# Row tile 0's scales loaded first, the identity added in PSUM by TensorE, the adapter product masked before its split

## What is computed

```
# block 1: a fake-quantised linear layer with a low-rank term
delta = lora_B @ lora_A * 0.5                      # 1024 x 1024, rank 64
wg    = (weight + delta) in groups of 128 columns
norm  = wg / exp(scale_log)                        # one scale per row and group
q     = cb[searchsorted(thresholds, norm)]         # 8 levels
w_eff = (((q - norm) + norm) * scale) + delta
x     = x + x @ w_eff.T
# block 2: gated MLP, F = 2752, with one adapter of rank 16 per sequence
gate  = x @ W_gate.T + 0.5 * (x @ A_gate[i].T) @ B_gate[i].T
up    = the same with W_up, A_up, B_up
down  = (silu(gate) * up) @ W_down.T + adapter
x     = x + down
```

## Time and profile before

| | |
|---|---|
| median of 3 runs | 1642.22 us (1639.8 to 1643.66) |
| the profiled execution | 1641.95 us, its span 1640.4 us |
| TensorE busy | 1595.8 us, 97% |
| VectorE busy | 1284.3 us, 78% |
| ScalarE busy | 572.9 us, 35% |
| GpSimd busy | 528.8 us, 32% |
| mean granted clock of TensorE | 0.99 |

### The profile page before, as it was taken

The page is one execution under the profiler, slowest core; times in us unless marked ns, Lnnn a source line. Parts: engine busy times, 40 slices in busy tenths (PEclk is TensorE's granted clock), DMA queues, the critical chain, the costliest instruction groups (busy, mean ns, idle before and its releaser), DMA issues.

```text
span 1640.4 us, 21380 instructions
## 1 busy us (share of the span) xinstructions
PE 1595.8 (97%) x7032; PEld 1300.8 (79%) x7032; DVE 1284.3 (78%) x1727; ACT 572.9 (35%) x1024; POOL 528.8 (32%) x399
## 2 busy tenths in 40 slices
PE   4999999999999999998999999999999999999999
PEld 3878887788888888766788888888778888888887
DVE  6899968788888899877887889999766576685353
ACT  4511125433333333345333333333343333233231
POOL 4230011355555555554444455556410000000000
PEclk8999999999999999998999999999999999999999
DMA  9473264466667777784446777876357777686563
GB/s 286 103 128 92 84 200 100 102 161 158 166 156 168 178 179 174 180 244 130 115 114 133 171 166 178 185 176 172 97 172 187 170 197 177 153 229 203 152 192 117
DMA packets 381452, 264.41 MB, mean 161 GB/s; under 512 B 228640, under 2 KB 302368, under 8 KB 381216
## 3 DMA queue, kind: packets, MB, share of 16 engines
q1 hardware_dynamic: 299072, 229.31, 53.8%
q10 hardware_dynamic: 80192, 27.94, 7.1%
q0 software_dynamic: 2080, 5.80, 1.8%
HBM read 167.84 MB, written 89.36 MB: 157 GB/s over the span
## 4 chain that ended last, share of the span: by engine, by line
PE 82%; DVE 14%; issue 2%; DMA 1%; ACT 1%; SPq 0%; DVEq 0%; ACTq 0%
PE bank L1746 20%; PE bankC L1746 14%; PE bankA L1746 14%; PE bank L1973 10%; PE bankA L1973 6%; PE bankC L1973 6%; PE bankT L1973 3%; DVE qsum L1542 2%; DVE xl L1257 1%; PE bankT L1793 1%; PE bankT L1794 1%; PE bankC L1758 1%; DVE qa L1527 1%; PE bank L1775 1%; DVE ts L1350 1%
## 5 line engine op out<-in xcount | busy, mean ns | idle before, releaser
L957 ACT CAST rh<-wt 128x512 fp32r<-128x512 f32 (+1 forms) x308 | 187.8, 611 | 446.3 <-PE bankA L1758 99.2
L1248 DVE TENSOR_TENSOR rl<-wt,rh 128x512 fp32r<-128x512 f32 (+1 forms) x308 | 280.9, 917 | 7.3 <-ACT rh L957 7.2
L1411 DVE TENSOR_TENSOR ll<-ll,lh 128x512 fp32r<-128x512 f32 (+1 forms) x154 | 108.2, 703 | 154.9 <-ACT lh L1066 154.4
L1746 PE MATMUL bank<-xh,rl 128*128 128x512 f32 (+1 forms) x528 | 205.7, 390 | 0.0
L1746 PE MATMUL bank<-xl,rh 128*128 128x512 f32 (+1 forms) x528 | 205.7, 390 | 0.0
L1746 PE MATMUL bank<-xh,rh 128*128 128x512 f32 (+1 forms) x528 | 205.7, 390 | 0.0
L1066 ACT CAST lh<-ll 128x512 fp32r<-128x512 f32 (+1 forms) x154 | 95.5, 621 | 269.4 <-DMA ll<-LT_d 264.1
L824 POOL TENSOR_TENSOR wt<-wt 128x512 f32<-128x512 f32 (+1 forms) x44 | 57.6, 1309 | 318.5 <-DVE wt L1242 318.5
L1746 PE MATMUL bankC<-xh,rh 128*128 128x512 f32 (+1 forms) x352 | 137.7, 391 | 2.2 <-DVE xl L1257 2.2
L1746 PE MATMUL bankC<-xl,rh 128*128 128x512 f32 (+1 forms) x352 | 137.8, 391 | 0.0
L1746 PE MATMUL bankC<-xh,rl 128*128 128x512 f32 (+1 forms) x352 | 137.7, 391 | 0.0
(11 more groups left out here) (207 smaller groups left out, 3597.6 us busy)
## 6 DMA issues: line engine op xcount, KB each, us to landing
ll<-LT_d SPq DMA_DIRECT2D x148, 256.0 KB, 2.9
wn<-in_L_cond_W_gate_dram SPq DMA_DIRECT2D x80, 256.0 KB, 5.4
wn<-in_L_cond_W_up_dram SPq DMA_DIRECT2D x80, 256.0 KB, 5.1
RT_d<-dt SPq DMA_DIRECT2D x70, 256.0 KB, 3.2
ql<-RT_d SPq DMA_DIRECT2D x70, 256.0 KB, 3.6
LT_d<-ev ACTq DMA_DIRECT2D x60, 256.0 KB, 2.6
dn<-in_L_cond_W_down_dram SPq DMA_DIRECT2D x86, 128.0 KB, 3.8
LT_d<-s2a SPq DMA_DIRECT2D x40, 256.0 KB, 4.2
```

The costliest lines, as they stand in the source:

```text
L957: nc.scalar.copy(rh[:, v % RING, 0:KH * rows], wsrc(RSRC[p], rows)).then_inc(s_hi, 1)
L1248: dv.tensor_tensor(rl[:, v % RING, 0:KH * rows], wsrc(RSRC[p], rows), rh[:, v % RING, 0:KH * rows].bitcast(f32), ALU.subtract).then_inc(s_ ...
L1411: dv.tensor_tensor(ll[0:rows, n % NL, :], ll[0:rows, n % NL, :].bitcast(f32), lh[0:rows, n % NL, :].bitcast(f32), ALU.subtract).then_inc(s ...
L1746: last = te.matmul(OUT[p][0:rows, :], a[:, u % RING, cols], b[:, OPND[p], k, :], start=k == 0 and n == 0, stop=k == KH - 1 and n == 2 and ...
```

## The change

- The transfers of `scale` are divided: row tile 0 first (`s_sc`, one transfer of 128 pieces of 32 bytes), tiles 1 to 7 after two token transfers (`s_scr`). The exponent and the reciprocal are divided in the same way; the second exponent stands in ScalarE's list after group 10, the second reciprocal inside `quantise(0)`. VectorE waits for the codebook alone before it builds the thresholds, and does the first eight of these steps ahead of the split of `lora_B`.
- `load_weight` is one transfer instead of four.
- `XFIRST` is 20 instead of 16.
- The identity is added by TensorE: `ident_add(o)` multiplies `minus2` (-2 times the identity) with `minus` in four matmuls of 32 columns into `bankD`, after VectorE has read `delta` for the quantisation and before it reads it for `eff` (new wait `s_idn`). It stands after group 12, at `g == 4` and then at `BUILD + LATER`. `QS` falls to 21.
- `LATER` is 12 for the tiles 1 to 6 and 5 for tile 7; `adapters_lo(o - 3)` stands at the beginning of `quantise(o)`; the adapters' stores are issued a tile later.
- The mask is applied in `ts_copy` (two pieces of 64x256) and `ts_sum`; `ts_hi` is four copies of 32x512 of which VectorE waits for two (`s_th`); `ts_lo` is two subtractions (`s_tlo`), and `ts_dup` on ScalarE copies them to the other two blocks. `ts_copy`, `ts_sum`, `ts_hi` and `ts_lo` of T(h, 0) stand one product earlier, `ts_hi` of T(h, 1) too.
- In the second pass `x_hi` and `x_lo` stand one product earlier.

The diff without its context and without the declarations of semaphores, indentation cut by eight:

```diff
+minus2 = place("minus2", [P, P], f32r, S0 + 75776)
...
-XFIRST = 2 * KD
-QS = 22
+XFIRST = 20
+QS = 21
...
-LATER = KD
+LATER = {o: 12 if o < KD - 1 else 5 for o in range(1, KD)}
...
         def load_weight(o):
-            for i in range(NI):
-                sp.dma_start(lw[i * Q:(i + 1) * Q, :], weight[i * DI + o * Q:i * DI + (o + 1) * Q, :]).then_inc(s_lw, 16)
+            sp.dma_start(lw[:, :], weight.rearrange("(i o r) d -> i o r d", i=NI, r=Q)[:, bass.ds(o, 1), :, :]
+                         .rearrange("i o r d -> i (o r) d")).then_inc(s_lw, 16)
-        for i in range(NI):
-            sp.dma_start(scale[i * Q:(i + 1) * Q, :, :],
-                         scale_log[i * DI:(i + 1) * DI].rearrange("(o r) g u -> r o (g u)", r=Q)).then_inc(s_cb, 16)
+        sp.dma_start(scale[:, 0, :], scale_log.rearrange("(i o r) g u -> i o r (g u)", i=NI, r=Q)[:, bass.ds(0, 1), :, :]
+                     .rearrange("i o r g -> i (o r) g")).then_inc(s_sc, 16)
         def load_nat(m):
...
+        for i in range(NI):
+            sp.dma_start(scale[i * Q:(i + 1) * Q, 1:KD, :],
+                         scale_log[i * DI + Q:(i + 1) * DI].rearrange("(o r) g u -> r o (g u)", r=Q)).then_inc(s_scr, 16)
...
-                if i == (BUILD[o] + LATER) // KD and o < KD - 1:
+                if i == (BUILD[o] + LATER[o]) // KD and o < KD - 1:
-                if i == (BUILD[o] + 28) // KD and o < KD - 1:
-                    store_adapters(o - 1)
+                if i == (BUILD[o] + 5) // KD and o > 1:
+                    store_adapters(o - 2)
...
-            nc.scalar.copy(tx[:, :], (bankC[:, 1, :], bank1[:, :])[t][2 * CR:4 * CR, :]).then_inc(s_tq, 1)
+            for b in range(CB):
+                part = slice(b * SEQ, (b + 1) * SEQ)
+                ins = nc.scalar.activation(tx[:, part], (bankC[:, 1, :], bank1[:, :])[t][2 * CR:4 * CR, part], ACT.Copy,
+                                           scale=half_of[2 * CR:4 * CR, b:b + 1])
+            ins.then_inc(s_tq, 1)
         def ts_hi(h, t):
...
-                g = slice(i % 2 * CR, (i % 2 + 1) * CR)
-                for b in range(CB):
-                    part = slice(b * SEQ, (b + 1) * SEQ)
-                    ins = nc.scalar.activation(ts[i * CR:(i + 1) * CR, t, i % 2, part], tx[g, part], ACT.Copy,
-                                               scale=half_of[g, b:b + 1])
-            ins.then_inc(s_tq, 1)
+                ins = nc.scalar.copy(ts[i * CR:(i + 1) * CR, t, i % 2, :], tx[i % 2 * CR:(i % 2 + 1) * CR, :])
+                if i == 1:
+                    ins.then_inc(s_th, 1)
+        def ts_dup(h, t):
+            act.wait_ge(s_tlo, 2 * h + t + 1)
+            for g in range(2):
+                ins = nc.scalar.copy(ts[(3 - g) * CR:(4 - g) * CR, t, g, :], ts[(1 - g) * CR:(2 - g) * CR, t, g, :].bitcast(f32))
+            ins.then_inc(s_ts, 1)
         def td_copy(h):
...
-        for i in range(NI):
-            act.dma_start(lw[i * Q:(i + 1) * Q, :], weight[i * DI:i * DI + Q, :]).then_inc(s_lw0, 16)
+        act.dma_start(lw[:, :], weight.rearrange("(i o r) d -> i o r d", i=NI, r=Q)[:, bass.ds(0, 1), :, :]
+                      .rearrange("i o r d -> i (o r) d")).then_inc(s_lw0, 16)
...
-        act.wait_ge(s_cb, 16 * (1 + NI))
-        nc.scalar.activation(scale[:, :, :], scale[:, :, :], ACT.Exp).then_inc(s_exp, 1)
+        nc.scalar.activation(minus2[:, :], ident[:, :], ACT.Copy, scale=-2.0).then_inc(s_neg1, 1)
+        act.wait_ge(s_sc, 16)
+        nc.scalar.activation(scale[:, 0, :], scale[:, 0, :], ACT.Exp).then_inc(s_exp, 1)
+            if u == KD + 2:
+                act.wait_ge(s_scr, 16 * NI)
+                nc.scalar.activation(scale[:, 1:KD, :], scale[:, 1:KD, :], ACT.Exp).then_inc(s_exp, 1)
...
-                    if g == BUILD[o] + LATER:
+                    if g == BUILD[o] + LATER[o] and o < KD - 1:
...
-            if 7 * (NM // 2) - 3 <= u < 7 * (NM // 2) + 4:
-                x_hi(1, u - 7 * (NM // 2) + 3)
+            if 7 * (NM // 2) - 4 <= u < 7 * (NM // 2) + 3:
+                x_hi(1, u - 7 * (NM // 2) + 4)
+            if mm in (0, NM // 2) and p in (2, 6):
+                ts_copy(mm // (NM // 2), p // 6)
-                ts_copy(mm // (NM // 2), p // 6)
+                ts_hi(mm // (NM // 2), p // 6)
-                ts_hi(mm // (NM // 2), 0)
+                ts_dup(mm // (NM // 2), 0)
-                ts_hi(mm // (NM // 2), 1)
+                ts_dup(mm // (NM // 2), 1)
...
         def ts_sum(h, t):
-            dve.wait_ge(s_tq, 2 * n + 1)
+            dve.wait_ge(s_tq, n + 1)
-            dv.tensor_tensor(tx[:, :], (bankC[:, 1, :], bank1[:, :])[t][0:2 * CR, :], tx[:, :], ALU.add).then_inc(s_tc, 1)
+            for b in range(CB):
+                part = slice(b * SEQ, (b + 1) * SEQ)
+                ins = dv.scalar_tensor_tensor(out=tx[:, part], in0=(bankC[:, 1, :], bank1[:, :])[t][0:2 * CR, part],
+                                              scalar=half_of[0:2 * CR, b:b + 1], in1=tx[:, part],
+                                              op0=ALU.mult, op1=ALU.add)
+            ins.then_inc(s_tc, 1)
         def ts_lo(h, t):
-            dve.wait_ge(s_tq, 2 * (2 * h + t) + 2)
-            block = [slice(i * CR, (i + 1) * CR) for i in range(4)]
-            for i in range(4):
-                g = (i + 1) % 2
-                for b in range(CB):
-                    part = slice(b * SEQ, (b + 1) * SEQ)
-                    ins = dv.scalar_tensor_tensor(out=ts[block[i], t, g, part], in0=tx[block[g], part],
-                                                  scalar=half_of[block[g], b:b + 1],
-                                                  in1=ts[block[g], t, g, part].bitcast(f32),
-                                                  op0=ALU.mult, op1=ALU.subtract)
-            ins.then_inc(s_ts, 1)
+            dve.wait_ge(s_th, 2 * h + t + 1)
+            for g in range(2):
+                mine = slice(g * CR, (g + 1) * CR)
+                ins = dv.tensor_tensor(ts[(1 - g) * CR:(2 - g) * CR, t, g, :], tx[mine, :], ts[mine, t, g, :].bitcast(f32),
+                                       ALU.subtract)
+            ins.then_inc(s_tlo, 1)
         def take_td(h):
...
-        dv.tensor_copy(la[0:RL, :], qsum[0:RL, :]).then_inc(s_lahi, 1)
-        dve.wait_ge(s_lahi, 1)
+        dv.tensor_copy(la[0:RL, :], qsum[0:RL, :]).then_inc(s_ophi, 1)
+        dve.wait_ge(s_ophi, 1)
-        dve.wait_ge(s_trL, 1)
-        dv.tensor_copy(lbT[:, 0, :], bankB(0)).then_inc(s_lb0, 1)
-        dve.wait_ge(s_lb0, 1)
-        lb_lo(0)
-        dve.wait_ge(s_cb, 16 * (1 + NI))
+        dve.wait_ge(s_cb, 16)
...
+        dve.wait_ge(s_trL, 1)
+        dv.tensor_copy(lbT[:, 0, :], bankB(0)).then_inc(s_ophi, 1)
+        dve.wait_ge(s_ophi, 2)
+        lb_lo(0)
         def t(i):
...
-        settle(dv.reciprocal(rscale[:, :, :].rearrange("p o g -> p (o g)"), scale[:, :, :].rearrange("p o g -> p (o g)")))
-        def quantise(o, early, mid, late):
+        settle(dv.reciprocal(rscale[:, 0, :], scale[:, 0, :]))
+        def quantise(o, begin, early, mid, late):
...
-                dve.wait_ge(s_lw0, 16 * NI)
+                dve.wait_ge(s_lw0, 16)
-                dve.wait_ge(s_lw, 16 * NI * o)
+                dve.wait_ge(s_lw, 16 * o)
+            begin()
...
-            n = QS - 6
+            n = QS - 5
...
+            dve.wait_ge(s_idn, o + 1)
-            for i in range(NI):
-                q = slice(i * Q, (i + 1) * Q)
-                dg = eff[q, i * DI + o * Q:i * DI + (o + 1) * Q]
-                ins = dv.tensor_tensor(dg, dg, ident[q, q], ALU.add)
-            chain(ins)
-            after(n + 6)
         def w_lo(o):
...
-        quantise(0, lambda: None, lambda: None, lambda: None)
+        def rest_of_scale():
+            dve.wait_ge(s_exp, 2)
+            settle(dv.reciprocal(rscale[:, 1:KD, :].rearrange("p o g -> p (o g)"),
+                                 scale[:, 1:KD, :].rearrange("p o g -> p (o g)")))
+        quantise(0, lambda: None, lambda: None, lambda: None, rest_of_scale)
+        def begin_of(o):
+            if o > 2:
+                adapters_lo(o - 3)
         def early_of(o):
...
         def late_of(o):
-            if o > 1:
-                adapters_lo(o - 2)
-            quantise(o, lambda: early_of(o), lambda: mid_of(o), lambda: late_of(o))
+            quantise(o, lambda: begin_of(o), lambda: early_of(o), lambda: mid_of(o), lambda: late_of(o))
+        adapters_lo(KD - 3)
...
+            if mm in (0, NM // 2) and p == 2:
+                ts_sum(mm // (NM // 2), 0)
-                ts_sum(mm // (NM // 2), 0)
-            if mm in (0, NM // 2) and p == 4:
-            if 7 * (NM // 2) - 2 <= u < 7 * (NM // 2) + 5:
-                x_lo(1, u - 7 * (NM // 2) + 2)
+            if 7 * (NM // 2) - 3 <= u < 7 * (NM // 2) + 4:
+                x_lo(1, u - 7 * (NM // 2) + 3)
...
+        def ident_add(o):
+            pe.wait_ge(s_dq, QS * o + 2)
+            for i in range(NI):
```

(22 more changed lines are left out.)

## The result

The changed kernel takes 1634.44 us (median of 6 runs, 1633.35 to 1638.07) against 1640.86 us of the kernel before beside it (6 runs, 1639.52 to 1643.66). The ratio is 0.9958, with an interval of 0.9945 to 0.9971. The prediction was 1615.2 with a range of 1609 to 1625. The direction was right and the time lies outside the range: three quarters of the forecast gain did not come.

A forecast was written before the change was run, and what follows sets the result against it. TensorE, busy throughout the long middle, was taken as the bound, so only what precedes or interrupts that stage counted. A 12.0 + B 9.5 + C 5.5 = 27.0 us off 1642.2 gave 1615.2 us, range 1609 to 1625.

The forecast's parts named there:

- A: Front and eight row tiles: earlier start and shorter VectorE work gain 9.4 + 3.2 - 0.6 = 12.0 us.
- R4: Row tiles: a ring of waits through VectorE, TensorE, ScalarE and SP closes; at 5 us a tile 1645 us; chance 0.05.
- The sum: Front to first BUILD step: TensorE reaches BUILD at 58.6 us with one identity add, 9.4 us earlier than before.
- B: Start of the second stage: both ts waits and the slow clock behind them go, gaining 9.5 us.
- The second chain: Second stage's start, second ts wait: copy to last copies takes about 7.7 us against three products, 8.2 us.
- 0.5 to spare: Second stage's start: margin in us of the ts chain (7.7) against three products (8.2), so the second wait goes.
- C: Second pass of the second stage: earlier operands and shorter ts work gain 5.5 us, between 2 and 10.
- R1: Front gives back its lead: tokens of groups 16 to 19 late, clock at half; 1620.8 us, chance 0.2.
- R2: Second stage: pass stays bound by transfers, or ts chain no shorter in B's second half; 1621.7 us, chance 0.12.
- R3: Second stage starts only when its operands' transfers are in, so A is worth nothing; 1627 us, chance 0.08.

The follow-up runs named there:

- e2: Changed kernel with weight tile 0 alone loaded by four transfers of 32 rows instead of one; 1626.51 us, ratio 0.9908.
- e6: Changed kernel with every weight tile loaded by four transfers of 32 rows again, all else kept; 1615.85 us, ratio 0.9844.
- e7: Changed kernel with weight tile 0 in one transfer of 128 adjacent rows instead of four blocks (wrong weights, same instructions); 1626.03 us, ratio 0.9908.
- e8: Kernel before with every weight tile loaded as one transfer in four blocks instead of four transfers; 1648.43 us, ratio 1.0047.
- f3: e6 with the identity added by VectorE behind eff again, no ident_add and no s_idn wait; 1616.15 us, ratio 0.9851.
- e9: e6 with XFIRST set back from 20 to 16; 1618.44 us, ratio 0.986.
- f1: e6 with lb of tile 2 issued by SP before the two last token transfers instead of behind them; 1614.53 us, ratio 0.9846.
- e3: Changed kernel with weight tile 0 in four transfers and the other scales' transfers issued before load_nat(2) and load_nat(3); 1627.64 us, ratio 0.992.
- f4: e6 with the second pass's x_hi and x_lo one product later, where the kernel before had them; 1618.58 us, ratio 0.9866.
- f2: e6 with lb of tiles 2 to 7 loaded by eight transfers of 32 rows instead of two of 128 rows; 1618.98 us, ratio 0.9867.

## Why the prediction was wrong

**The step that failed** is in part A: "The codebook was issued near 2.9 and needed 6.1 us, so it is there at 9.0." The 6.1 us are a row of the kernel before, read as if a landing time belonged to a transfer. It depends on what else is under way: the codebook needed 17.6 us in the changed kernel. The change touched that: I wrote "the weight of a tile comes in one DMA instead of four, on queues nobody waits for" and looked only at who waits for the weight (and even there VectorE waits 1.8 us, in e2 6.5). But the load on ScalarE's queue holds up those on SP's: `lb`, codebook and exponents, for which everybody waits, run beside it. With that transfer taken back (e6) the codebook is there at 9.5, `quantise(0)` starts at 14.0 and `lora_delta(1)` at 35.70 (forecast 13.6 and 35.4).

The Trainium skill has the rule that I missed (DMA: Bandwidth & Descriptors, Why a DMA increments its semaphore by 16 and not by 1): a transfer is spread over as many of the 16 DMA engines as divide the slowest dimension of both of its patterns; its list Rules for kernel authors says to put a multiple of 16 outermost. The new source is `[4, 32, 1024]`, so by the page four engines; an estimate from it is 128 KB for each of these, against 32 KB for each of 16 in the old form. e2, e6, e7 and e8 all agree, with 182 GB/s against 384. The traces don't say which engine moved a packet, but they have every packet's start and duration, and the 128 of weight tile 0 can be told by their 4096 bytes on ScalarE's queue. In the changed kernel they run from 3.1 to 13.5 us, never more than 6 at once and exactly four for 73% of that time. In e2 they run from 2.0 to 7.0 and in e7 from 1.9 to 4.2, with up to 18 at once; in e8, again in blocks, from 3.5 to 12.9 with at most 6.

**One bad pattern, three places.** Weight tile 0 delays the start. Weight tile 1 delays `lb` of tile 2, which TensorE needs before the main loop (4.8 us in the changed kernel, 11.2 in e2), and behind that wait the granted clock is 0.50 from 56 to 60 us. The other weight tiles slow the adapters' stores: tile 4 is issued at 104.3, a store right behind it at 105.9 needs 15.6 us, and the next 8.7. In the changed kernel, 100 to 135 us:

```profile
BdT_d<-bd_st SPq DMA_DIRECT2D x2, 64.0 KB, 12.1
```

and in e6, 90 to 125 us:

```profile
BdT_d<-bd_st SPq DMA_DIRECT2D x2, 64.0 KB, 4.5
```

This closes rival R4's ring once: `adapters_hi` waits 8.8 us for the store, `out_x1` stands behind it in ScalarE's queue, and TensorE waits 1.7 us for `x1t_st`. In e6 0.3 is left of it. I had given the store "2 to 3 us" and never asked what else would be under way.

**The rest of A.** The clock stayed at 1.00 through the longer stretch of transposes, as forecast (here the changed kernel, 36 to 40 us, transposes and products with `minus`):

```profile
36.00:40.00 4.00, 4.00 (x25) 2.65 (x23) 3.97 (x4) 4.00 (x10) 0.00 (x0) 1.00 1.06 333
```

The rule of the Trainium skill weighed in the prediction (TensorE: Matmul & The Clock Gate, Part 4: PE-mode transpose) would have had it fall; in this mix it did not. In e6 `lora_delta(1)` too comes at full clock and takes 1.11 us:

```profile
35.70 1.11 PE L1841 MATMUL bank<-la,lbT 128*128 128x512 f32 x4
```

In the changed kernel it does not. It comes only at 46.13 and takes 1.67, behind three pauses of half a microsecond or less, and the clock is below 1.00 there; why is open:

```profile
44.00:48.00 4.00, 2.87 (x8) 1.82 (x9) 2.10 (x5) 2.30 (x5) 0.00 (x0) 0.83 0.57 129
```

The identity add takes 0.35 us for four matmuls (I took 0.4), 0.09 each. The Trainium skill (TensorE: Matmul & The Clock Gate, Back-to-back issue gap) gives about 0.06 only for a sequencer with hardware decode off, and 0.025 otherwise, a condition that I left out; the measured 0.09 lies above both. A tile takes 23.78 us (151.64 to 175.42) against 23.88; I had said 24.05, having taken 23.65 for TensorE's own work where it is 0.2 less. So TensorE did become the bound, as said, but the move of the identity is worth nothing (f3). Inside the main loop A gained 5.5 us, 206.75 to 201.25 (e6). 2.4 of them lie ahead of the first BUILD step (21.8 to 19.4) and are the four groups less an identity add. The other 3.1 lie behind it (184.9 to 181.8); e9 and f3 have them as well (181.8 and 182.1), so they come neither from the groups nor from the identity. What else moved in the row tiles, `LATER` and `adapters_lo`, was not tried alone. The sum had 58.6 for BUILD, which doesn't follow from its own terms: 40.0, 21.8 as before, 2.7 less and 0.4 more give 59.5. Measured are 19.4 us from the first product, where the sum had 18.6.

A's total, forecast as 12.0, is 9.5 in e6, where the unforeseen wait of 3.5 for `lb` of tile 2 remains, and 13.0 in f1 without it, of which about 1.3 are f1's luckier front.

**B** was right: both `ts` waits gone, `T` 5.72 instead of 7.10 (I had 5.4), the product behind them 2.77 instead of 3.86. The second chain was worked out at 7.7 us; in the changed kernel it runs from 287.7 to 295.7, 8.0 us, against products until 295.8. The "0.5 to spare" is 0.1. The wait of 2.0 in e3 is the first of the two, so neither margin is wide.

**C** was right in the main and 2 us too small: T(1, 1) starts 22.0 us behind the end of the product ahead of T(1, 0), instead of 25.8: 3.8 nearer (3.5 forecast). 1.0 of it is lost again ahead of the pass, where TensorE now waits longer for `ad`, first before, then changed:

```profile
730.79 0.50 PE L1793 MATMUL bankT<-ah,ad 96*128 96x512 f32 x1 [0.36 <-DVE ad L1375]
731.01 0.50 PE L1817 MATMUL bankT<-ah,ad 96*128 96x512 f32 x1 [1.37 <-DVE ad L1395]
```

A `ts` wait of 0.7 remains, but `T` takes 5.72 instead of 7.30. I had counted nothing for the clock, because TensorE would still wait for VectorE in that pass. It does, 3.1 us, and `T` is fast all the same.

**The rivals.** R1 and R2 name waits that didn't come. R3, that the front's lead is lost at the second stage's transfers, is refuted: the rest column is 1370.7 to 1371.4 in seven kernels, whether the second stage starts at 239.9 or at 263.7; where it is more, a wait for `ts`, f4's holes or, in e9, a slower product behind the wait for `xl` stand behind it. R4's ring is real, but at 1.7 us once.

What stays open: why e7's `lb` comes 5.3 us later than e2's (the order of issue fits and wasn't tried alone), how much each of the three places costs by itself, and what gave the 3.1 us behind BUILD.

## What to carry to other kernels

Fewer transfers are not always cheaper ones. When a load's form changes, read both access patterns' outermost dimension and ask what runs beside it, not only who waits for it. A landing time from a trace holds only as long as its neighbours in all queues stay the same: where a change touches a large transfer, bound the small ones around it by the large one's time. If the DMA engines' busy share is near 1 and the GB/s are half of what the same stretch had before, suspect a transfer on too few engines, and count how many of its packets are under way at once.

## What was not expected of the hardware

- A 512 KB load whose source is four blocks of 32 rows holds all DMA traffic at 182 GB/s from 8 to 12 us and delays a 4 KB load, issued 2 us behind it on another queue, from 6.1 to 17.6 us. The same bytes in four transfers, or from 128 adjacent rows, run at 368 to 384.
- A choked DMA shows on the issuing side too: SP needed 12.85 us to issue two token loads in the changed kernel, 2.64 in e2.
- For 32 KB the same pattern did no harm that more transfers could mend: with eight instead of two the wait for `lb` of tile 2 was 4.9 us instead of 3.5, and the kernel 3.1 us slower (f2).
- The clock does not fall behind every wait of this length. In e6 TensorE waited 3.5 us before the first product and the clock stayed at 1.00; in f4 it waited 3.2 us at the same place, and from 40 to 42 us the clock is

```profile
40.00:42.00 2.00, 2.00 (x9) 1.90 (x8) 1.81 (x4) 1.25 (x3) 0.00 (x0) 0.50 0.76 226
```

  The first product then takes 0.78 us instead of 0.48.
